# A ranking tower on one core: rounds of eight feature units with one run of sums, in place of two rounds of four

## The chip, the core and the metric

The kernel runs on one core of a Trainium2 chip. The metric is the device time of one execution in microseconds (us). Five engines of the core matter here, each with its own instruction stream: TensorE (PE in the rows, its weight loads PEld), VectorE (DVE), ScalarE (ACT), GpSimd (POOL) and SyncE (SP). They meet through semaphores: an instruction can wait for a count and raise one when it ends.

## The reference, cut to what matters

A batch of 1024 rows; for each row 32 fields are looked up in 32 tables, each entry 64 wide. All 496 pairs of fields are combined through a 64x64 matrix per pair, and a small network follows:

```python
e = jnp.stack([tbl_0[ids[:, 0]], ..., tbl_31[ids[:, 31]]], axis=1)   # 1024 x 32 x 64
p, q = e[:, iu, :], e[:, ju, :]                                       # 496 pairs, iu < ju
z = jnp.einsum('bpe,fpe,bpf->bp', p, kernel, q)                       # 1024 x 496
h = jnp.concatenate([z, dense_ctx], axis=1)                           # 1024 x 512
h = jnp.maximum(h @ W_top1 + b_top1, 0.0)                             # 512 -> 512
h = jnp.maximum(h @ W_top2 + b_top2, 0.0)                             # 512 -> 256
y = h @ W_top3                                                        # 256 -> 1
```

All is 32-bit floating point.

## The kernel before, in words

**Tiles and units.** The batch is cut into 8 tiles of 128 rows. GpSimd gathers the fields (L356), TensorE transposes them into feature layout (a "fill", L611) and ScalarE copies the transposes to `xt` (L394). The pairs of a tile are computed in 32 units of three kinds, all of which take one of three places (`TRING = 3`) in the PSUM ring `t_ps`:

- 16 feature units F (L570): eight matmuls with the pair matrices as weights give the transformed field with features on partitions. VectorE multiplies by the partner field (L476) and writes to a place of `prod`. The sum over the features is still to be made, and lies across partitions: TensorE makes it with matmuls against a matrix of zeros and ones, `sel_sb` (L642, "the sums"), into `z_ps`.
- 8 cross units C (L600) and 8 batch units B (L587), with the batch on partitions. VectorE multiplies them (L498; L517 and L533) into a place of the ring `prod_a`; here the sum lies along a row, and ScalarE makes it (L418), or VectorE (L504), or in the last tile for the C units GpSimd (L374), into `zb`.

The later network is computed for two tiles at a time: `zb` is transposed (L626, "the turn"), then seven "pieces" of matmuls follow (L657, L704, L710), spread between units of later tiles.

**What sets the order.** A table written by the program, `SCHEDULE`, fixes TensorE's instruction order: units, fills, turns, pieces and sums. In tiles 4 to 6 the units run C, F, B, F, eight times over; in tiles 0 to 3 they are sorted by the field that arrives last; in tile 7 they run C, B, F eight times, then the other eight F. ScalarE has its own table made from the same one. VectorE follows the units.

**The sums before the change.** Four F units are a round (`BURST = 4`), so a tile has four rounds and the program 32. The sums of a round are 16 matmuls in a row (L638 to L646), placed five units after the round's last unit (three in the first two tiles), since TensorE first waits for VectorE's products (L632). Those of the last round stand inside the last layers (L670). TensorE's matmul with 32-bit operands shows as two records in the trace, so a run of 16 matmuls is 32 records (x32).

**The places.** `prod` has `FRING = 8` places, two rounds. VectorE, before the first unit of a round, waits for the sums of the round that used these places (L475). `prod_a` has 7 places: a C or B unit waits for the sums of the unit seven before it (L484 to L492). The ring `t_ps` makes TensorE wait, before a unit, for VectorE's product of the unit three before it (L557). `prep_ps` is one buffer for fills, turns and pieces: each waits until ScalarE has copied the one before it (L616, L684).

Of the kernel before, what the change touches and what calls it, by code (L numbers as in the profile page):

```python
# [16 lines left out]
RING = 12  # L17
XRING = 2 * PACKS
TRING = 3
ARING = 7  # L20

# [6 lines left out]
F_UNITS = [x for n, x in enumerate(_UNITS) if n % 3 != 1]  # L30
B_UNITS = [(g, part) for g in range(GROUPS) for part in range(2)]
NF, NC, NBU = len(F_UNITS), len(CROSS_UNITS), len(B_UNITS)
NU = NF + NC + NBU
BURST = 4
FRING = 2 * BURST


def gather_after(t, field):
# [4 lines left out]

ROUNDS = NF // BURST
LAST = TILES * ROUNDS
# [175 lines left out]
TURN_OF = {who: a for a, who in enumerate(TURNS)}  # L221
# [46 lines left out]
def build(nc, ids, tables, kmat, dense, w1, b1, w2, b2, w3, sel, ident, y):  # L268
# [3 lines left out]
    with ctx:  # L272
# [17 lines left out]
        prod = sb("prod", [P, FRING, 2, W])  # L290
        prod_a = sb("prod_a", [P, ARING, 2, W])
        zb = sb("zb", [P, TILES, 2 * P])
# [16 lines left out]
        t_done, prod_done, summed, z_copied = sem("t_done"), sem("prod_done"), sem("summed"), sem("z_copied")  # L309
# [7 lines left out]
        def slot_of(t, k):  # L317

            return (t * PACKS + k) % XRING
# [23 lines left out]
        def _(pool):  # L343
# [17 lines left out]
            for unit in POOL_COUNT:  # L361

                cells, begin = side_cells(unit)
                products = prod_a[:, NTH[unit] % ARING].rearrange("p n (c w) -> p (n c) w", w=EMBED)
                pool.wait_ge(prod_done, COUNT[unit])
# [12 lines left out]
        def _(act):  # L378
# [32 lines left out]
            def sum_bank(*who):  # L411
# [3 lines left out]
                for f in range(cells):  # L415
                    product = prod_a[:, NTH[unit] % ARING, n, f * EMBED:(f + 1) * EMBED]
                    at = begin + n * cells + f
# [49 lines left out]
        @block.vector  # L467
        def _(dve):
            def feature_multiply(t, u):
                r = t * ROUNDS + u // BURST  # L470
                slot, own, here = TURN_OF["F", t, u] % TRING, (t * NF + u) % FRING, slot_of(t, F_UNITS[u][0])
                if r >= 2 and u % BURST == 0:

                    dve.wait_ge(summed, r - 1)
                dve.wait_ge(t_done, COUNT["F", t, u])  # L475
                nc.vector.tensor_tensor(prod[:, own].rearrange("p n (m b) -> p (n m) b", b=P),  # L476
                                        t_ps[:, slot].rearrange("p n (m b) -> p (n m) b", b=P),
                                        xt[:, here:here + 1, :].broadcast_to([P, 2 * GROUP, P]),
                                        ALU.mult).then_inc(prod_done, 1)

            def side_slot(unit):

                n = NTH[unit]
                if n >= ARING:  # L484

# [50 lines left out]
            for unit in UNITS:  # L536
                kind, t, u = unit
# [262 lines left out]
```

## Time and profile before

| | |
|---|---|
| device time, median of 3 runs | 483.64 us (479.96 to 483.74) |
| the profiled execution: its own time | 483.11 us |
| the profiled execution: span of its instructions | 481.3 us |
| granted TensorE clock, mean | 0.957 |
| PE busy | 411.4 us, 85% of the span |
| DVE busy | 342.4 us, 71% |
| ACT busy | 325.4 us, 68% |
| POOL busy | 268.3 us, 56% |

The busy time is a mean over stages: in the first 55 us the tables and matrices arrive and the engines have gaps; from about 57 us to the end TensorE hardly rests. "Idle before" is the time an engine stood still before an instruction and what ended it; "issue" there means that nothing the profile shows was waited for.

### The profile page before, as it was taken

Reading aid. Unit: us, or ns where it says so; the run is one execution under the profiler, and the core shown is the slowest. Engines: PE = TensorE matmul, PEld = TensorE weight load, DVE = VectorE, ACT = ScalarE, POOL = GpSimd, SP = SyncE. Lnnn points to the kernel's source line nnn. Section 1 sums busy time; section 2 is a strip of 40 time slices with the busy share of each in tenths; the row PEclk is TensorE's granted clock in tenths of the full one; section 3 lists DMA queues with packets and bytes.
Section 4 is the critical chain, followed back from the end, with each engine's and each line's share of the span. In section 5 each row is a group of like instructions: output and inputs, shape, how many; then the busy total and the mean of one; then the engine's idle time right before and its main releaser. Section 6 shows DMA issues by size and latency. Waiting matters only on the chain.

```text
span 481.3 us, 12047 instructions
## 1 busy us (share of the span) xinstructions
PE 411.4 (85%) x4144; PEld 280.4 (58%) x4144; DVE 342.4 (71%) x428; ACT 325.4 (68%) x2456; POOL 268.3 (56%) x308
## 2 busy tenths in 40 slices
PE   0554358888898988999999999999999999999997
PEld 0332245655556555767666666666666566666875
DVE  0044158889798878788778887888888788877820
ACT  1244215078967887689857897878786978988512
POOL 5757735566556555555545555556555555577400
PEclk9976568999998999999999999999999999999999
DMA  8751101015111111111111111111111111000000
GB/s 278 268 215 27 26 14 24 18 24 155 21 23 21 20 24 21 21 22 22 23 19 20 23 23 21 20 24 21 20 24 23 22 21 20 16 1 3 1 2 0
DMA packets 12756, 19.17 MB, mean 40 GB/s; under 512 B 6036, under 2 KB 6296, under 8 KB 12568
## 3 DMA queue, kind: packets, MB, share of 16 engines
q0 software_dynamic: 8192, 8.40, 9.4%
q1 hardware_dynamic: 2592, 8.29, 4.8%
q10 hardware_dynamic: 1912, 1.71, 1.2%
q8 instruction: 33, 0.54, 0.5%
q14 instruction: 27, 0.22, 0.1%
HBM read 18.39 MB, written 0.00 MB: 38 GB/s over the span
## 4 chain that ended last, share of the span: by engine, by line
PE 74%; DVE 12%; issue 9%; another core or an unknown queue 2%; DMA 2%; POOL 1%; ACT 1%; DVEq 0%
PE t_ps L570 25%; PE z_ps L642 14%; PE t_ps L600 12%; PE t_ps L587 9%; DVE prod L476 6%; PE prep_ps L657 5%; PE prep_ps L611 3%; DVE prod_a L498 2%; PE prep_ps L704 2%; DVE prod_a L517 2%; PE t_ps L657 2%; DVE zb L504 1%; DMA raw<-tbl,ids_sb 1%; POOL raw L356 1%
## 5 line engine op out<-in xcount | busy, mean ns | idle before, releaser
L356 POOL DMA_INDIRECT raw<-tbl,ids_sb x256 | 242.3, 946 | 172.5 <-issue 48.0
L418 ACT ACTIVATE prod_a<-prod_a 128x64 f32<-128x64 f32 x1184 | 283.9, 243 | 69.0 <-DVE prod_a L533 33.5
L418 ACT ACTIVATION_READ_ACCUMULATOR prod_a<-prod_a 128x1 f32 x1184 | 223.9, 189 | 7.5 <-issue 7.5
L476 DVE TENSOR_TENSOR prod<-t_ps,xt 128x1024 f32<-128x1024 f32 x128 | 155.7, 1220 | 63.6 <-PE t_ps L570 25.5
L570 PEld LDWEIGHTS t_ps<-xt,k_sb 64*128 64x128 f32 x2048 | 136.5, 193 | 55.3 <-issue 31.7
L570 PE MATMUL t_ps<-xt,k_sb 64*128 64x128 f32 x2048 | 151.7, 286 | 19.3 <-issue 10.1
L498 DVE TENSOR_TENSOR prod_a<-t_ps,raw 128x1024 f32<-128x1024 f32 x64 | 78.0, 1219 | 23.6 <-PE t_ps L600 14.7
L600 PE MATMUL t_ps<-k_sb,xt 64*128 64x512 f32 x256 | 74.7, 654 | 19.3 <-issue 14.1
L517 DVE TENSOR_TENSOR prod_a<-t_ps,raw 128x768 f32<-128x768 f32 (+2 forms) x96 | 62.9, 683 | 31.1 <-PE t_ps L587 24.0
L642 PE MATMUL z_ps<-prod,sel_sb 128*32 128x256 f32 x1024 | 71.7, 390 | 4.0 <-issue 3.7
L587 PE MATMUL t_ps<-k_sb,xt 64*128 64x384 f32 (+5 forms) x448 | 66.0, 402 | 3.5 <-issue 1.8
L642 PEld LDWEIGHTS z_ps<-prod,sel_sb 128*32 128x32 f32 x1024 | 33.9, 111 | 39.0 <-issue 22.6
L587 PEld LDWEIGHTS t_ps<-k_sb,xt 64*128 64x128 f32 x448 | 43.0, 191 | 21.9 <-issue 9.6
L394 ACT ACTIVATE xt<-prep_ps 128x512 f32<-128x512 f32 (+2 forms) x47 | 21.0, 446 | 42.6 <-PE prep_ps L611 31.0
L504 DVE TENSOR_REDUCE zb<-prod_a 128x8 f32<-128x512 f32 x76 | 49.7, 676 | 0.0
L611 PE MATMUL prep_ps<-ident_sb,raw 128*128 128x128 f32 x128 | 26.4, 305 | 20.8 <-DMA raw<-tbl,ids_sb 15.1
L600 PEld LDWEIGHTS t_ps<-k_sb,xt 64*128 64x128 f32 x256 | 21.0, 191 | 32.5 <-issue 23.7
L611 PEld LDWEIGHTS prep_ps<-ident_sb,raw 128*128 128x128 f32 x128 | 14.3, 144 | 38.0 <-issue 25.8
L374 POOL TENSOR_TENSOR prod_a<-prod_a 128x512 f32<-128x512 f32 (+4 forms) x40 | 24.3, 607 | 9.7 <-DVE prod_a L498 7.2
L533 DVE TENSOR_TENSOR prod_a<-t_ps,raw 128x128 f32<-128x128 f32 x64 | 18.0, 281 | 0.0
L657 PE MATMUL prep_ps<-zbt,w_sb 128*128 128x256 f32 x48 | 13.6, 405 | 0.0
L657 PE MATMUL prep_ps<-zt,w_sb 128*128 128x256 f32 x48 | 12.3, 379 | 0.0
(30 smaller groups left out, 91.1 us busy)
## 6 DMA issues: line engine op xcount, KB each, us to landing
raw<-tbl,ids_sb POOLq DMA_INDIRECT x256
k_sb<-kmat SPq DMA_DIRECT2D x4, 768.0 KB
k_sb<-kmat SPq DMA_DIRECT2D x4, 512.0 KB
k_sb<-kmat SPq DMA_DIRECT2D x4, 448.0 KB, 4.6
k_sb<-kmat SPq DMA_DIRECT2D x4, 256.0 KB
w_sb<-w ACTq DMA_DIRECT2D x1, 1024.0 KB
w_sb<-w ACTq DMA_DIRECT2D x1, 512.0 KB
ids_sb<-ids SPq DMA_DIRECT2D x1, 128.0 KB, 2.4
```

Source lines behind the costliest of these rows:

```text
L356: nc.gpsimd.indirect_dma_start(raw[:, n % RING, begin:begin + EMBED], None, tables[2 * k + f], bass.IndirectOffsetOnAxis(ap=ids_sb[:, t, 2 ...
L418: last = nc.scalar.activation(product, product, ACT.Copy, accum_out=zb[:, unit[1], at:at + 1])
L476: nc.vector.tensor_tensor(prod[:, own].rearrange("p n (m b) -> p (n m) b", b=P), t_ps[:, slot].rearrange("p n (m b) -> p (n m) b", b=P), x ...
L498: nc.vector.tensor_tensor(out, product, rows.unsqueeze(1).broadcast_to([P, 2, W]), ALU.mult).then_inc(prod_done, 1)
L504: nc.vector.tensor_reduce(zb[:, unit[1], begin + n * cells:begin + (n + 1) * cells], prod_a[:, NTH[unit] % ARING, n, 0:cells * EMBED].rear ...
L517: return nc.vector.tensor_tensor(out[:, :, cols], product[:, :, cols], rows[:, fields * EMBED:(fields + cells) * EMBED].unsqueeze(1).broad ...
L570: last = nc.tensor.matmul(t_ps[:, slot, n, i * P:(i + 1) * P], k_sb[rows, cols], xt[rows, x, :], start=True, stop=True)
L587: last = nc.tensor.matmul(product[:, n, cell * EMBED:(cell + cells) * EMBED], xt[rows, slot_of(t, GROUP * g + field // 2), :], k_sb[rows, ...
L600: last = nc.tensor.matmul(product[:, n, :], xt[rows, slot_of(t, k), :], k_sb[rows, COL["C", k, j]], start=True, stop=True)
L611: last = nc.tensor.transpose(prep_ps[:, n * P:(n + 1) * P], raw[:, group % RING, at * P:(at + 1) * P], ident_sb[:])
L642: last = nc.tensor.matmul(z_ps[32 * group:32 * group + 32, 0:ZBLOCKS * P], sel_sb[:, 30 - 2 * pos:62 - 2 * pos], prod[:, (t * NF + u) % FR ...
L657: return nc.tensor.matmul(out, w1_sb[:, part, m * P:(m + 1) * P], z, start=(part == ZBLOCKS), stop=(part == ZBLOCKS - 1 and half != 0))
```

## The change

A round is now eight F units, so a tile has two rounds and the program 16, each with one run of 32 matmuls. `prod` has 12 places in place of 8, `prod_a` 5 in place of 7 (a place of either is 4 KB per partition). The wait for free places of `prod` is written for a ring that isn't a whole number of rounds: VectorE waits at the 13th F unit and then at every eighth, for the round whose places it is about to reuse.

```diff
@@ constants
-ARING = 7
+ARING = 5
...
-BURST = 4
-FRING = 2 * BURST
+BURST = 8
+FRING = 12
@@ feature_multiply, on VectorE
-                r = t * ROUNDS + u // BURST
-                slot, own, here = TURN_OF["F", t, u] % TRING, (t * NF + u) % FRING, slot_of(t, F_UNITS[u][0])
-                if r >= 2 and u % BURST == 0:
+                n = t * NF + u
+                slot, own, here = TURN_OF["F", t, u] % TRING, n % FRING, slot_of(t, F_UNITS[u][0])
+                if n >= FRING and (n == FRING or n % BURST == FRING % BURST):
 
-                    dve.wait_ge(summed, r - 1)
+                    dve.wait_ge(summed, (n - FRING) // BURST + 1)
```

`ROUNDS`, `LAST` and `ROUND_DONE` follow from `BURST`, and with them `SCHEDULE`. The instructions of VectorE, ScalarE, GpSimd and SyncE stand in the same order; only TensorE's move.

On TensorE in tile 4, before the change, each quarter of a tile has its run of sums (x16) behind a C unit (L600, x2):

```order
L611 MATMUL prep_ps<-ident_sb,raw 128x128 x4
L600 MATMUL t_ps<-k_sb,xt 128x512 x2
L642 MATMUL z_ps<-prod,sel_sb 32x256 x16
L570 MATMUL t_ps<-xt,k_sb 128x128 x8
L587 MATMUL t_ps<-k_sb,xt 128x192
L587 MATMUL t_ps<-k_sb,xt 128x128
L587 MATMUL t_ps<-k_sb,xt 128x256
L587 MATMUL t_ps<-k_sb,xt 128x320
L570 MATMUL t_ps<-xt,k_sb 128x128 x8
```

and now, in the first and then the second quarter of the half tile:

```order
L600 MATMUL t_ps<-k_sb,xt 128x512 x2
L642 MATMUL z_ps<-prod,sel_sb 32x256 x32
L570 MATMUL t_ps<-xt,k_sb 128x128 x8
```

```order
L611 MATMUL prep_ps<-ident_sb,raw 128x128 x4
L600 MATMUL t_ps<-k_sb,xt 128x512 x2
L570 MATMUL t_ps<-xt,k_sb 128x128 x8
L587 MATMUL t_ps<-k_sb,xt 128x192
L587 MATMUL t_ps<-k_sb,xt 128x128
```

Every second run has gone from its place and stands, as 16 more matmuls, in the run that comes two quarters of units later, at the place where the odd rounds had theirs.

At the end of TensorE's stream, before (the turn L626, then the sums of the last round but one, then the last piece of the third pair of tiles L710):

```order
L626 MATMUL prep_ps<-ident_sb,zb 128x128 x4
L642 MATMUL z_ps<-prod,sel_sb 32x256 x16
L710 MATMUL prep_ps<-h,w_sb 1x256 x2
```

```order
L642 MATMUL z_ps<-prod,sel_sb 32x256 x16
L657 MATMUL t_ps<-zt,w_sb 128x128 x8
```

and now:

```order
L626 MATMUL prep_ps<-ident_sb,zb 128x128 x4
L710 MATMUL prep_ps<-h,w_sb 1x256 x2
L657 MATMUL t_ps<-zbt,w_sb 128x256 x2
```

```order
L642 MATMUL z_ps<-prod,sel_sb 32x256 x32
L657 MATMUL t_ps<-zt,w_sb 128x128 x8
```

The run that stood between the turn and L710 is now part of the last one, before the last layers.

## Rows read from the trace of the kernel before

**Rows 1.** The page: busy times, the instruction queue, shares of the chain that ended last.
```profile
PE 411.4 (85%) x4144; PEld 280.4 (58%) x4144; DVE 342.4 (71%) x428; ACT 325.4 (68%) x2456; POOL 268.3 (56%) x308
...
q8 instruction: 33, 0.54, 0.5%
...
PE 74%; DVE 12%; issue 9%; another core or an unknown queue 2%; DMA 2%; POOL 1%; ACT 1%; DVEq 0%
```

**Rows 2.** Busy time in eight quarters (stretch, length, engines' busy us, clock, DMA).
```profile
264.00:277.00 13.00, 12.03 (x132) 7.93 (x134) 11.39 (x15) 10.87 (x84) 7.69 (x9) 1.00 0.11 23
...
sum 105.00, PE 99.61 PEld 69.24 DVE 86.83 ACT 85.55 POOL 60.51; mean PE 12.45 PEld 8.66 DVE 10.85 ACT 10.69 POOL 7.56
```

**Rows 3.** Timeline of PE (start us, length us, line, operation, tiles, records [idle before]).
```profile
258.19 1.13 PE L600 MATMUL t_ps<-k_sb,xt 64*128 64x512 f32 x4
259.16 1.06 PE L570 MATMUL t_ps<-xt,k_sb 64*128 64x128 f32 x16
...
263.16 1.13 PE L600 MATMUL t_ps<-k_sb,xt 64*128 64x512 f32 x4 [0.61 <-DVE prod L476]
264.22 1.93 PE L642 MATMUL z_ps<-prod,sel_sb 128*32 128x256 f32 x32
266.08 0.71 PE L570 MATMUL t_ps<-xt,k_sb 64*128 64x128 f32 x6
267.71 0.81 PE L570 MATMUL t_ps<-xt,k_sb 64*128 64x128 f32 x9 [0.92 <-issue]
```

**Rows 4.** The line of the sums: shortest, median, longest record in ns.
```profile
L642 PE MATMUL z_ps<-prod,sel_sb x1024: 376/379/634, 67.1 to 471.7; 128*32 128x256 f32 x171
```

**Rows 5.** Timeline of PE, at two runs of even rounds.
```profile
329.84 2.73 PE L642 MATMUL z_ps<-prod,sel_sb 128*32 128x256 f32 x32
332.50 1.16 PE L570 MATMUL t_ps<-xt,k_sb 64*128 64x128 f32 x16
...
382.23 3.08 PE L642 MATMUL z_ps<-prod,sel_sb 128*32 128x256 f32 x32
385.25 1.16 PE L570 MATMUL t_ps<-xt,k_sb 64*128 64x128 f32 x16
```

**Rows 6.** Timeline of DVE at a run of sums.
```profile
265.27 1.22 DVE L476 TENSOR_TENSOR prod<-t_ps,xt 128x1024 f32<-128x1024 f32 x1
266.40 1.22 DVE L498 TENSOR_TENSOR prod_a<-t_ps,raw 128x1024 f32<-128x1024 f32 x1
268.67 1.22 DVE L476 TENSOR_TENSOR prod<-t_ps,xt 128x1024 f32<-128x1024 f32 x1 [1.05 <-PE t_ps L570]
```

**Rows 7.** Timeline of PE in tile 0, at the first two runs of sums.
```profile
67.11 2.41 PE L642 MATMUL z_ps<-prod,sel_sb 128*32 128x256 f32 x32
...
76.96 1.13 PE L600 MATMUL t_ps<-k_sb,xt 64*128 64x512 f32 x4 [2.25 <-issue]
...
81.75 1.93 PE L642 MATMUL z_ps<-prod,sel_sb 128*32 128x256 f32 x32
```

**Rows 8.** Timeline of PE at the end.
```profile
454.13 1.93 PE L642 MATMUL z_ps<-prod,sel_sb 128*32 128x256 f32 x32
...
461.44 0.66 PE L626 MATMUL prep_ps<-ident_sb,zb 128*128 128x128 f32 x4 [0.57 <-ACT h L436]
462.02 1.93 PE L642 MATMUL z_ps<-prod,sel_sb 128*32 128x256 f32 x32
463.77 1.03 PE L710 MATMUL prep_ps<-h,w_sb 128*1 128x256 f32 x4
```

**Rows 9.** ScalarE's copy of the turned sums, by tile (shortest, median, longest ns).
```profile
L401 ACT ACTIVATE zbt<-prep_ps x4: 571/587/597, 177.9 to 462.1; 128x512 f32<-128x512 f32 x4
```

**Rows 10.** Timeline of DVE, the last F units.
```profile
456.14 4.62 DVE L476 TENSOR_TENSOR prod<-t_ps,xt 128x1024 f32<-128x1024 f32 x4 [0.89 <-PE z_ps L642]
```

**Rows 11.** ScalarE's last sum of a B unit; DVE's product five C and B units later.
```profile
111.72 0.18 ACT L418 ACTIVATION_READ_ACCUMULATOR prod_a<-prod_a 128x1 f32 x1
...
114.69 1.22 DVE L498 TENSOR_TENSOR prod_a<-t_ps,raw 128x1024 f32<-128x1024 f32 x1
```

## The prediction, made before the changed kernel ran

> **What bounds the kernel now.** I read the page first: TensorE is busy for 411 of 481 us and holds 74% of the chain that ended last, VectorE 12% [rows 1]. The shares are means over stages, so the next view is the busy time by stretch. Between 264 and 369 us lie eight quarters of a tile, 13.1 us each (105 / 8). In one, TensorE is busy 12.45 us, VectorE 10.85, ScalarE 10.69 [rows 2]. TensorE is the bound, but VectorE is only 2.3 us behind it, and this gap is about as long as the part of a quarter in which TensorE does sums and therefore makes nothing for VectorE. That is what the reader should keep in mind: the two engines share a ring of three places, and the sums are the breathing space of one and a pause of the other.
>
> The timeline of TensorE shows a run of sums in detail [rows 3]. It starts 1.06 us after the start of the C unit ahead of it; an F unit behind a C unit starts after 0.97 us (258.19 to 259.16). The first record of the run and the last are 1.93 - 0.38 = 1.55 us apart [rows 3, 4], so 0.050 us from one to the next, and the next F unit starts 1.86 us after the run's start. 32 records at 0.050 are 1.60 us; 0.26 us more pass before the F unit starts. So a run costs 1.60 us of work, 0.26 us to get out and 0.09 us to get in.
>
> There is a third thing, which the profile does not explain. Close behind the start of a run TensorE stands still for most of a microsecond, with nothing waited for ("issue"): here 0.92 us after the first six records of the F unit [rows 3], in other runs in the middle of the sums, which then take 2.66 us (329.84 to 332.50) or 3.02 us (382.23 to 385.25) in place of 1.86 [rows 5], so 0.80 and 1.16 us too long. I call it the hiccup. Of the runs between 264 and 411 us each has one; the runs of tiles 2 and 3 that stand behind a B unit have little of it, and the runs from 421 us on none, as 454.13 and 462.02 show [rows 8].
>
> **The change part by part.** Sixteen runs of 32 matmuls replace 32 of 16. The matmuls, their weight loads and all other instructions stay.
>
> *Getting in and out.* Each merged pair saves 0.26 + 0.09 = 0.35 us. Fourteen pairs lie between tile 0 and the tail, where TensorE sets the pace: 14 x 0.35 = 4.9 us. For this the trace agrees with a rule of the Trainium skill (TensorEngine Tiling (Array Packing), Tiling Modes) that changing the tiling mode drains TensorE; the sums are 128 rows by 32 columns and the units 64 by 128. The page gives no figure for that. TensorE: Matmul & The Clock Gate (Single matmul latency, the Trainium skill) has about 0.175 us for an unhidden drain; by that figure alone the estimate of this term would be 14 x 0.175 = 2.5 us, and by the rows it is 4.9.
>
> *The hiccups.* The runs that go are those of even rounds. Eight of them carry a hiccup, of 0.98 us in the mean of the two shown [rows 5]. If it belongs to the run, eight go: 7.8 us. If it belongs to a number of instructions, none goes. A doubled run could also have two. The ends are thus 7.8 us and nothing. I take 7.8, because in tile 4 to 6 each hiccup stands within 40 records of a run's start, and where no run is near there is none of that length.
>
> *What VectorE gives back.* Without its run and its hiccup a quarter costs TensorE 13.1 - 1.86 - 0.98 = 10.3 us. VectorE needs 10.85 [rows 2]. TensorE can be no more than three units ahead, and is already at that limit when the next sums come: the C unit ahead of them waited 0.61 us for VectorE's product [rows 3]. So the quarter without sums goes at VectorE's pace, 10.85 - 10.27 = 0.58 us longer. In the eight half tiles where a hiccup goes, that is 4.6 us back. In the others the quarter keeps more than 10.85 us of TensorE's work, and nothing is given back. The ends: nothing, if VectorE's slack evens out, and what the last rival below says.
>
> *The first pair.* The first run, at 67.11, costs nothing now: at 76.96 TensorE waits 2.25 us for something that arrives, and would wait longer without the run. Its 32 records move to 81.75 and stand on the path there [rows 7]: +1.6 us.
>
> *The tail.* The run between the turn (L626) and L710 goes. L710 writes the buffer that ScalarE copies after the turn, and the copy takes 0.59 us [rows 9]. Now the run hides it: from the turn's start to L710 are 2.33 us (461.44 to 463.77) [rows 8]. After the change they are the turn's 0.66, the copy's 0.59 and two hand-overs, which I take as 0.05 each: 1.35 us, 0.98 less. The 32 records stand in the last run instead, +1.6 us. Together +0.6 us. The run at 454.13 doubles too, and VectorE's last four products wait for its end, as now with 0.89 us [rows 10]; they are needed only by the very last run, over 9 us later (456.14 + 4.62 = 460.8 against 470), so that costs nothing while this cover of 9 us holds.
>
> *The places.* VectorE's wait for `prod` never holds it longer than TensorE does, since the sums stand at least two units ahead of the unit that waits for them, and VectorE needs those two units anyway; the exception is the one at the end, above. Queued behind that waiting product are VectorE's last three alone. With 5 places in place of 7 a product needs ScalarE's sums of the unit five before it. The narrowest place is in tile 1: the sum ends at 111.90 and the product starts at 114.69, 2.8 us later [rows 11]; in tiles 4 to 6 there are some 10 us. The cost is nothing; if the cover went, ScalarE's 10.69 us a quarter would come in as a third bound, still under VectorE's.
>
> *The sum.* -4.9 - 7.8 + 4.6 + 1.6 + 0.6 = -5.9 us, on the profiled execution's own 483.1: 477.2. The median of the three runs is 0.5 us above that execution, so I forecast 477.7 us.
>
> **The rivals.** About 1% (4.8 us) is what a measurement can tell from no change: under 478.8 is faster, over 488.5 slower.
>
> 1. *The hiccup comes once in so many instructions.* Their number does not change, so none goes, and the quarters without sums keep 11.2 us of TensorE's work, over VectorE's 10.85: nothing is given back either. -4.9 + 2.2 = -2.7: 480.9 us. For it: 33 packets of instructions of 16 KB were loaded [rows 1], about one for each of the 32 runs. Against: all runs from 421 us on have none. The Trainium skill (Runtime: NRT & Kernel Launch, Instruction fetch mechanics) says that code comes in such blocks of 256 instructions and that the cost of crossing into one is mostly hidden; the trace agrees on the blocks and can't say whether they are the hiccups. Chance 0.24.
>
> 2. *VectorE gives nothing back.* Its 2.3 us of idle time a quarter could let it work off what TensorE piles up, since TensorE's halt during the doubled run comes later but is longer. -4.9 - 7.8 + 2.2 = -10.5: 473.1 us. For it: over the eight quarters TensorE waits for VectorE but a few tenths each. Against: that wait stands just where the next sums stood. Chance 0.15.
>
> 3. *VectorE starves in the long run* (the one on the other side). At a run's start three units lie ready for it; from 264.22 to 267.62 (266.40 + 1.22) it has work, 3.4 us [rows 3, 6]. Now sums of 1.86 and the next unit's 1.1 are 2.96 us: covered, and the idle 1.05 at 268.67 [rows 6] is the hiccup's. After the change, 1.86 + 1.60 + 1.1 = 4.56 us: 1.16 us are uncovered. This decides if VectorE, and not TensorE, sets the time between the runs all along, that is, if the pause in TensorE's output is longer than 3.4 us and the ring is full before each. Then thirteen half tiles lose 1.16 us each, 15.1, and 7.8 of hiccups and the getting in and out are all that speaks against it: 15.1 - 7.8 + 2.2 = +9.5: 493.1 us. Against: VectorE's 10.85 leave 2.3 us of each quarter. Chance 0.14.
>
> 4. *Five places are too few*, so that VectorE waits for ScalarE: by rows 11 it would take a ScalarE 2.8 us later than now. Chance 0.03, some 486 us. That the change does not do what it says is excluded by TensorE's order, which has the 16 runs.
>
> **How the numbers follow.** My forecast has 0.38, and 0.06 is for what I don't see. The range of the forecast alone is 474 to 481 (half of the hiccups, or half of what is given back). To hold eight in ten it must take in rivals 1 and 2 and leave out most of 3: 471 to 487. Faster by over 1%: rival 2 and some two thirds of the forecast, 0.42. Within 1%: rival 1 and the rest of the forecast, 0.42. Slower: rival 3 and a little of the unseen, 0.16.
>
> **What would show it.** In the changed profile: a run of 64 records whose first and last start about 3.15 us apart, one per half tile; a hiccup at each of them and none in the quarters between (right for the second term), or one there too (rival 1); in the quarters without sums TensorE's idle time ahead of C units "until DVE prod" grown to over half a microsecond (the give-back); VectorE idle once per half tile for some 2 us, waiting for TensorE. ScalarE's sums must not show up as what VectorE waits for. At the end L710 should start 1.35 us after the turn. I am wrong if hiccups are longer in long runs, or if VectorE's idle time as a whole grows.

## The result, and the profile after

The changed kernel takes 497.0 us (median of 4 runs, 496.26 to 497.60), the kernel before in the same session 483.25 us (4 runs, 479.96 to 483.74). The ratio is 1.032, with a 95% interval of 1.029 to 1.035: 3.2% slower. I had forecast 477.7 us and a range up to 487.

The page of the changed kernel, in lines that answer to [rows 1]:

```profile
span 495.8 us, 12034 instructions
PE 414.8 (84%) x4144; PEld 282.8 (57%) x4144; DVE 340.6 (69%) x428; ACT 325.8 (66%) x2456; POOL 267.6 (54%) x308
PE 68%; DVE 15%; issue 10%; POOL 4%; DMA 2%; ACT 0%; DVEq 0%; another core or an unknown queue 0%
```

Of its groups the one of VectorE's feature products, before and then now (line, engine, operation, count | busy us, mean ns | idle us before it and what ended most of that):

```profile
L476 DVE TENSOR_TENSOR prod<-t_ps,xt 128x1024 f32<-128x1024 f32 x128 | 155.7, 1220 | 63.6 <-PE t_ps L570 25.5
L476 DVE TENSOR_TENSOR prod<-t_ps,xt 128x1024 f32<-128x1024 f32 x128 | 155.5, 1219 | 76.1 <-PE t_ps L570 40.1
```

The work is the same, and no engine's busy time grew by more than 1%. What grew is idle time: on TensorE from 69.9 to 81.0 us (the span less its busy time), on VectorE from 138.9 to 155.2. Of VectorE's, this group had 63.6 us before the change, 25.5 of them until an F unit, and has 76.1 and 40.1 now. In the same stretch as [rows 2], 264 to 369 us, less work gets done by both engines, 82.43 us of VectorE's against 86.83:

```profile
sum 105.00, PE 97.92 PEld 67.10 DVE 82.43 ACT 83.54 POOL 57.66; mean PE 48.96 PEld 33.55 DVE 41.21 ACT 41.77 POOL 28.83
```

The timeline of TensorE over one half tile, which answers to [rows 3]:

```profile
271.81 5.40 PE L642 MATMUL z_ps<-prod,sel_sb 128*32 128x256 f32 x64
277.14 1.16 PE L570 MATMUL t_ps<-xt,k_sb 64*128 64x128 f32 x16
...
288.82 1.03 PE L587 MATMUL t_ps<-k_sb,xt 64*128 64x192 f32 x8 [0.66 <-DVE prod L476]
...
293.44 1.16 PE L570 MATMUL t_ps<-xt,k_sb 64*128 64x128 f32 x16 [0.68 <-DVE prod_a L533]
...
296.53 1.16 PE L570 MATMUL t_ps<-xt,k_sb 64*128 64x128 f32 x16 [0.88 <-issue]
...
299.27 4.68 PE L642 MATMUL z_ps<-prod,sel_sb 128*32 128x256 f32 x64
```

One run of 64 records per half tile is there, but it takes 5.33 us to the next unit (271.81 to 277.14) and then 4.61, where 3.6 would do (the same run takes 3.59 us in after_again, below): the hiccups did not go, they stand inside the doubled runs. Between the runs TensorE waits for VectorE at 288.82 and 293.44. The gap at 296.53 is called "issue", but it ends 0.06 us after VectorE's product of the C unit three units before (from 295.25 to 296.47), and that product had itself waited 0.73 us for ScalarE's sums of `prod_a`. The timeline of VectorE in the same half tile, answering to [rows 6]:

```profile
274.19 1.22 DVE L498 TENSOR_TENSOR prod_a<-t_ps,raw 128x1024 f32<-128x1024 f32 x1
278.35 1.22 DVE L476 TENSOR_TENSOR prod<-t_ps,xt 128x1024 f32<-128x1024 f32 x1 [2.94 <-PE t_ps L570]
```

VectorE stands still for 2.94 us at this run and for 2.95 at the next (305.09): once per half tile, until the F unit behind the sums.

### The profile page after: what moved, and what is told of

Its sections match the earlier page's. It is cut to its first block, busy times and chain, and to the rows that moved or that the text cites. A ratio compares the mean times of both kernels' runs of the same rounds, so it can differ in the third digit from the quotient of the medians.

```text
span 495.8 us, 12034 instructions
## 1 busy us (share of the span) xinstructions
PE 414.8 (84%) x4144; PEld 282.8 (57%) x4144; DVE 340.6 (69%) x428; ACT 325.8 (66%) x2456; POOL 267.6 (54%) x308
## 4 chain that ended last, share of the span: by engine, by line
PE 68%; DVE 15%; issue 10%; POOL 4%; DMA 2%; ACT 0%; DVEq 0%; another core or an unknown queue 0%
PE t_ps L570 22%; PE z_ps L642 14%; PE t_ps L600 13%; PE t_ps L587 7%; DVE prod L476 7%; PE prep_ps L657 4%; DVE prod_a L498 4%; PE prep_ps L611 3%; POOL raw L356 3%; DVE zb L504 2%; PE prep_ps L704 2%; DVE prod_a L517 2%; POOL prod_a L374 2%; PE t_ps L657 2%; DMA raw<-tbl,ids_sb 1%
## 5 line engine op out<-in xcount | busy, mean ns | idle before, releaser
L418 ACT ACTIVATE prod_a<-prod_a 128x64 f32<-128x64 f32 x1184 | 283.8, 243 | 71.7 <-DVE prod_a L533 32.3
L418 ACT ACTIVATION_READ_ACCUMULATOR prod_a<-prod_a 128x1 f32 x1184 | 223.9, 189 | 8.8 <-issue 8.8
L476 DVE TENSOR_TENSOR prod<-t_ps,xt 128x1024 f32<-128x1024 f32 x128 | 155.5, 1219 | 76.1 <-PE t_ps L570 40.1
L570 PEld LDWEIGHTS t_ps<-xt,k_sb 64*128 64x128 f32 x2048 | 133.0, 195 | 61.1 <-issue 29.2
L570 PE MATMUL t_ps<-xt,k_sb 64*128 64x128 f32 x2048 | 149.5, 288 | 19.3 <-issue 6.7
L600 PE MATMUL t_ps<-k_sb,xt 64*128 64x512 f32 x256 | 75.0, 664 | 25.3 <-issue 19.1
L587 PE MATMUL t_ps<-k_sb,xt 64*128 64x384 f32 (+4 forms) x448 | 65.7, 408 | 9.1 <-DVE prod L476 7.7
L642 PE MATMUL z_ps<-prod,sel_sb 128*32 128x256 f32 x1024 | 68.7, 382 | 5.0 <-issue 3.9
L587 PEld LDWEIGHTS t_ps<-k_sb,xt 64*128 64x128 f32 x448 | 42.8, 192 | 27.5 <-DVE prod L476 11.0
L642 PEld LDWEIGHTS z_ps<-prod,sel_sb 128*32 128x32 f32 x1024 | 37.9, 109 | 34.0 <-issue 20.2
L504 DVE TENSOR_REDUCE zb<-prod_a 128x8 f32<-128x512 f32 x76 | 49.7, 676 | 0.0
L394 ACT ACTIVATE xt<-prep_ps 128x512 f32<-128x512 f32 (+2 forms) x47 | 20.9, 445 | 40.6 <-PE prep_ps L611 19.5
L600 PEld LDWEIGHTS t_ps<-k_sb,xt 64*128 64x128 f32 x256 | 20.0, 191 | 40.1 <-issue 30.0
L409 ACT ACTIVATE zt<-z_ps 128x256 f32<-128x256 f32 x8 | 3.1, 384 | 17.6 <-PE z_ps L642 17.5
```

The lines of the kernel that those rows point to most:

```text
L418: last = nc.scalar.activation(product, product, ACT.Copy, accum_out=zb[:, unit[1], at:at + 1])
L504: nc.vector.tensor_reduce(zb[:, unit[1], begin + n * cells:begin + (n + 1) * cells], prod_a[:, NTH[unit] % ARING, n, 0:cells * EMBED].rear ...
L570: last = nc.tensor.matmul(t_ps[:, slot, n, i * P:(i + 1) * P], k_sb[rows, cols], xt[rows, x, :], start=True, stop=True)
L587: last = nc.tensor.matmul(product[:, n, cell * EMBED:(cell + cells) * EMBED], xt[rows, slot_of(t, GROUP * g + field // 2), :], k_sb[rows, ...
L600: last = nc.tensor.matmul(product[:, n, :], xt[rows, slot_of(t, k), :], k_sb[rows, COL["C", k, j]], start=True, stop=True)
L642: last = nc.tensor.matmul(z_ps[32 * group:32 * group + 32, 0:ZBLOCKS * P], sel_sb[:, 30 - 2 * pos:62 - 2 * pos], prod[:, (t * NF + u) % FR ...
```

## The experiments

They ran later, in groups on four chips, and this matters for two things. On each of the four the kernel before takes 420.5 to 421.5 us, not 483; I call the chip of the first profiles, which has no number on record, the first chip, and these the later chips. And their profiles have next to no hiccups: of the runs of sums between 100 and 400 us only one is too long, by 0.78 us (in before_light_both, at 177.90). So the readings of the hiccups (H1 to H4 where an expectation names them) could not be told apart. The loss could be studied: its ratio is about the same, 1.032 on the first chip and 1.028 later, with intervals that overlap. All ratios are to the kernel before on the same chip, with 95% intervals; times of different groups differ by up to 1 us for the same kernel, so between groups I compare ratios. The ideas to be told apart are that the long pause in TensorE's output starves VectorE (my rival 3; A in the expectations), that a ring is too short or that the hiccups grew (both called B there), that the long run costs TensorE something by itself (C, and later E), and that ScalarE's copy of the finished sums holds the other engines up (D).

**The changed kernel again** (after_again), with no edit.

> The changed kernel again, beside the others. Theory A (VectorE stands still in the doubled run; TensorE's unexplained halts have little part in the loss): 1.027 to 1.032 of the kernel before, also where the profile shows no halts. Theory B (the halts grew in the doubled runs and make the loss): with no halts in the profile the ratio falls under 1.02.

432.58 us, ratio 1.028 [1.025, 1.031]. Its timelines of TensorE, then of VectorE:

```profile
296.69 3.66 PE L642 MATMUL z_ps<-prod,sel_sb 128*32 128x256 f32 x64
300.28 1.16 PE L570 MATMUL t_ps<-xt,k_sb 64*128 64x128 f32 x16
...
320.89 3.66 PE L642 MATMUL z_ps<-prod,sel_sb 128*32 128x256 f32 x64
```

```profile
298.24 1.22 DVE L498 TENSOR_TENSOR prod_a<-t_ps,raw 128x1024 f32<-128x1024 f32 x1
301.49 1.22 DVE L476 TENSOR_TENSOR prod<-t_ps,xt 128x1024 f32<-128x1024 f32 x1 [2.04 <-PE t_ps L570]
...
306.20 1.22 DVE L498 TENSOR_TENSOR prod_a<-t_ps,raw 128x1024 f32<-128x1024 f32 x1 [0.63 <-PE t_ps L600]
...
316.79 1.22 DVE L498 TENSOR_TENSOR prod_a<-t_ps,raw 128x1024 f32<-128x1024 f32 x1 [0.33 <-PE t_ps L600]
```

The runs are clean (3.66 us), and the kernel is slower by about the same share as on the first chip, as A expected. The hiccups are not needed for the loss. VectorE waits 2.04 us at the run; then, from 306.20 to 316.45, it has no gap at all: the quarter without sums goes at VectorE's pace. It shows on TensorE and VectorE side by side:

```profile
311.40 1.03 PE L587 MATMUL t_ps<-k_sb,xt 64*128 64x192 f32 x8
312.53 1.16 PE L570 MATMUL t_ps<-xt,k_sb 64*128 64x128 f32 x16
```

```profile
310.13 1.21 DVE L476 TENSOR_TENSOR prod<-t_ps,xt 128x1024 f32<-128x1024 f32 x1
311.26 1.21 DVE L498 TENSOR_TENSOR prod_a<-t_ps,raw 128x1024 f32<-128x1024 f32 x1
```

Each of the two units starts 0.06 us after VectorE's product of the unit three before it (which ends at 311.34 and 312.47), since only then is its place in `t_ps` free. The half tile takes 24.20 us (296.69 to 320.89).

**The places.** Two kernels: rounds of four with the new rings and the new wait (b4_f12_a5), and the changed kernel with the old 7 places of `prod_a`, paid for with the ring of gathered fields (b8_a7_raw8).

```diff
@@ against the kernel before; the wait at L475 is the changed kernel's, too
-ARING = 7
+ARING = 5
...
-FRING = 2 * BURST
+FRING = 12
```

> The changed kernel with rounds of four again, so 32 runs of 16 matmuls, but its rings kept: 12 places for prod, 5 for prod_a. Theory A (the doubled run is the loss: VectorE uses up its three waiting units and then stands still): the time of the kernel before, 483.3 us, within 1.5. Theory B (five places are too few, VectorE waits for ScalarE): most of the loss stays, 490 to 497 us.

421.19 us, 0.999 [0.998, 1.000], as A expected. The rings and the wait alone cost nothing.

```diff
@@ against the changed kernel
-RING = 12
+RING = 8
...
-ARING = 5
+ARING = 7
```

> The changed kernel with 7 places for prod_a again; room for them comes from the ring of gathered rows, 8 groups in place of 12. Theory A: 494 to 497 us, since the 3.5 us in which VectorE waits for ScalarE in the changed kernel's profile are mostly given back by TensorE's halt. Theory B: about 485 us. If it is slower than 497, the smaller ring of gathered rows costs something itself.

432.64 us, 1.028 [1.025, 1.030], the same as the changed kernel. So the places of `prod_a` are not the cause. Whether 12 places of `prod` are too few for rounds of eight no run tests, but the trace answers it: in after_again VectorE waits for TensorE's sums (L642) not once between 40 and 400 us, and in the changed kernel on the first chip once, for 2.6 us. What is left is the length of the rounds. b4_f12_a5 also shows what a half tile is with rounds of four, on TensorE:

```profile
255.10 1.93 PE L642 MATMUL z_ps<-prod,sel_sb 128*32 128x256 f32 x32
...
266.99 1.93 PE L642 MATMUL z_ps<-prod,sel_sb 128*32 128x256 f32 x32
...
278.88 1.94 PE L642 MATMUL z_ps<-prod,sel_sb 128*32 128x256 f32 x32
```

23.78 us (255.10 to 278.88), 0.42 less than with the doubled run, although TensorE has one run more to get in and out of.

That is not yet the whole loss, which is 10.4 us between these two profiles. Where it arises is seen from the start of the F unit behind the same run of sums in both, counted in doubled runs. after_again is 0.3 us behind at the first (in tile 0), 4.0 at the fourth (in tile 2), 5.6 at the eighth (in tile 4), 9.8 at the 14th (in tile 7) and 10.4 at the end. In the six half tiles from the eighth run to the 14th it loses 0.42 or 0.43 us in four, and 1.25 in each of the two that have the turn (L626).

**Two pauses close together, no longer run** (b4_lag7). The kernel before, with its sums seven units behind the round in place of five.

```diff
-SUMS_LAG = 5
+SUMS_LAG = 7
```

> The kernel before with its sums two units later (SUMS_LAG 7 in place of 5), so in tiles 4 to 6 each run stands behind a B unit and not behind a C unit. Theory H3 (a halt appears where the instructions ahead of the run are few and fast, since the runs of tiles 2 and 3 behind a B unit had little of it): the halts shrink in tiles 4 to 6, 472 to 478 us. Theory H4 (the halt belongs to the run or to time, wherever it stands): 482 to 485 us.

433.41 us, 1.028 [1.026, 1.031]. It was made to sort out the hiccups, and neither H3 nor H4 foresaw a loss; the reading that follows came after the result. TensorE, then VectorE:

```profile
274.91 1.93 PE L642 MATMUL z_ps<-prod,sel_sb 128*32 128x256 f32 x32
276.78 1.16 PE L570 MATMUL t_ps<-xt,k_sb 64*128 64x128 f32 x16
277.87 1.13 PE L657 MATMUL prep_ps<-zbt,w_sb 128*128 128x256 f32 x4
278.83 1.03 PE L657 MATMUL prep_ps<-zt,w_sb 128*128 128x256 f32 x4
279.79 1.13 PE L600 MATMUL t_ps<-k_sb,xt 64*128 64x512 f32 x4
```

```profile
277.99 1.23 DVE L476 TENSOR_TENSOR prod<-t_ps,xt 128x1024 f32<-128x1024 f32 x1
281.04 1.23 DVE L498 TENSOR_TENSOR prod_a<-t_ps,raw 128x1024 f32<-128x1024 f32 x1 [1.83 <-PE t_ps L600]
```

The sums (1.87 us) and the piece (1.92 us) now have a single F unit between them, and VectorE waits 1.83 us behind them. Runs, their number and all rings are as before, and the loss is as large as that of the change. That the two are equal is chance: here the first two tiles lose nothing, since their sums did not move, and in tile 5 two quarters take 25.16 us (274.91 to the run at 300.07) against 23.78. What costs is a stretch in which TensorE makes little for VectorE, whatever fills it.

**Gathers left out in tiles 4 to 7** (before_nogather4), aimed at the hiccups.

```diff
+GATHERED = 4
...
+                if t >= GATHERED:
+                    continue
```

TensorE's wait for these gathers goes with them.

> The kernel before without the gathers of tiles 4 to 7 (it leaves them out and computes those tiles from rows that older tiles left); TensorE's instructions are the same but for the waits for them. Theory H1 (TensorE's halts without a releaser, 0.8 to 1.2 us behind each run of sums from 264 to 411 us, come from something the gathers do, since the runs after the gathers' end have none): those halts are gone in tiles 4 to 6, some 11 us less, about 472 us. Theory H2 (they belong to TensorE's own stream of instructions, its code blocks or its queue): they stay, 481 to 484 us.

421.08 us, 0.999 [0.997, 1.001]. There were no hiccups on its chip to take away, so it decides nothing on them. It shows that in tiles 4 to 7 the gathers do not bound.

**VectorE made lighter** (before_light_dve and after_light_dve). The same edit in both: VectorE's 76 row sums (L504, 49.7 us in all) become additions of one element per cell.

```diff
-                nc.vector.tensor_reduce(zb[...], prod_a[...], mybir.AxisListType.X, ALU.add)
+                first = prod_a[...][:, :, 0:1]
+                nc.vector.tensor_tensor(zb[...].unsqueeze(2), first, first, ALU.add)
```

> The kernel before with VectorE's 76 row sums (L504, 0.65 us each) replaced by a sum over one element of each cell, which takes them out of the result. Theory A: TensorE sets the pace before the change, so the 45 us less of VectorE's work shorten the program by little: 0.97 to 1.0 of the kernel before.

> The same in the changed kernel. Theory A (the loss is VectorE's: its work between the doubled runs and its pause in them): with VectorE 1.3 us lighter per quarter TensorE alone sets the pace, the doubled runs save 0.35 us each, and this kernel is no slower than before_light_dve, from 6 us faster to 1 us slower. Theory C (the loss is TensorE's own, in the long run itself): it stays about 12 us slower than before_light_dve.

413.88 us, 0.982 [0.978, 0.986], and 418.91 us, 0.995 [0.991, 0.998]. With a lighter VectorE the doubled rounds lose 5.0 us in place of 12.0 (432.58 less the 420.53 of the kernel before in this group): about 7 are VectorE's. Neither reading came true: A expected at most 1 us of loss, C 12. The kernel before gains 7 too, so VectorE bounded it in part already.

The other 5 us can be read in the same profile. TensorE's waits between 40 and 400 us that ScalarE ended, and one of them in tile 4, at the fill behind a turn:

```profile
PE prep_ps L610 <- ACT zbt L401: 2.7, 3, 1.4
PE prep_ps L610 <- ACT xt L394: 2.7, 3, 1.9
```

```profile
236.29 0.66 PE L610 MATMUL prep_ps<-ident_sb,raw 128*128 128x128 f32 x4 [1.38 <-ACT zbt L401]
```

With the smaller ones these waits are 7.6 us, against 2.3 in before_light_dve. `prep_ps` is one buffer, and each fill waits until ScalarE has copied what was in it; ScalarE's copies (L394, L401) stand in its queue between its row sums, and come late. In tiles 4 to 6 after_light_dve wins 0.08 or 0.09 us in each of the four half tiles without a turn and loses 1.72 and 1.44 in the two with one.

**ScalarE lighter as well** (before_light_both and after_light_both): ScalarE's row sums (L418) also become one copy of one element per cell.

```diff
-                for f in range(cells):
-                    last = nc.scalar.activation(product, product, ACT.Copy, accum_out=zb[...])
+                nc.scalar.activation(zb[...].unsqueeze(2), first, ACT.Copy)
```

> The kernel before with the row sums of VectorE and of ScalarE both replaced (VectorE: a sum over one element of each cell; ScalarE: one copy of one element of each cell), which leaves these sums out of the result. TensorE is then the only busy engine: a few us under before_light_dve, 405 to 413.

> The same in the changed kernel. Theory A+ (TensorE's saving of 0.35 us per merged pair is real, and what turned it into a loss are VectorE and ScalarE, both too busy to make up a long pause): 1 to 5 us faster than before_light_both (sum of TensorE's terms: -4.9 + 2.2 = -2.7). Theory E (the price per run is not real, or the doubled run costs TensorE something by itself): 0 to 4 us slower.

411.65 us, 0.979 [0.976, 0.981], and 412.02 us, 0.980 [0.978, 0.982]. The two are equal: with light partners the loss is gone. But the gain that I had priced does not come either: A expected 1 to 5 us, and 0.4 us slower lies in E's range. In part this is the early tiles, where with light partners TensorE waits for gathered fields (2.2 us at 174.89 in before_light_both alone): from the seventh run to the 15th the changed kernel is 0.9 to 1.2 us ahead. Half tiles of TensorE, first of before_light_both, then of after_light_both (the lines of the kernel are three lower here):

```profile
234.11 1.93 PE L639 MATMUL z_ps<-prod,sel_sb 128*32 128x256 f32 x32
...
257.88 1.50 PE L639 MATMUL z_ps<-prod,sel_sb 128*32 128x256 f32 x23
```

```profile
255.15 3.66 PE L639 MATMUL z_ps<-prod,sel_sb 128*32 128x256 f32 x64
258.74 1.16 PE L567 MATMUL t_ps<-xt,k_sb 64*128 64x128 f32 x16
259.74 0.93 PE L584 MATMUL t_ps<-k_sb,xt 64*128 64x192 f32 x8
260.49 1.06 PE L567 MATMUL t_ps<-xt,k_sb 64*128 64x128 f32 x16
...
268.67 1.06 PE L567 MATMUL t_ps<-xt,k_sb 64*128 64x128 f32 x16
269.56 0.93 PE L584 MATMUL t_ps<-k_sb,xt 64*128 64x192 f32 x8
270.47 1.16 PE L567 MATMUL t_ps<-xt,k_sb 64*128 64x128 f32 x16
...
278.84 1.50 PE L639 MATMUL z_ps<-prod,sel_sb 128*32 128x256 f32 x24
```

23.77 us against 23.69: 0.08 saved per half tile, not 0.35. The merged run takes 3.59 us (255.15 to 258.74), 0.13 less than two of 1.86; a C unit without a run behind it takes 0.09 less, and an F unit without a run ahead of it takes 0.89 (268.67 to 269.56) in place of 1.00 (258.74 to 259.74). That is 0.33 in all. But 0.25 of it is lost again in the quarter without sums, which takes 10.17 us (268.67 to 278.84) where 11.89 - 1.86 - 0.11 = 9.92 would be due. It can be seen: the B unit of 269.56 takes 0.91 us to the F unit behind it, the same kind at 259.74 only 0.75, and that F unit 1.09 to the piece at 271.56, in place of 1.00 (260.49 to 261.49). The F unit at 270.47 starts 0.05 us after VectorE's product of the C unit three before it ends (at 270.42), so TensorE is still held by VectorE here. VectorE's timeline at the run:

```profile
255.68 1.22 DVE L496 TENSOR_TENSOR prod_a<-t_ps,raw 128x1024 f32<-128x1024 f32 x1
259.95 1.22 DVE L474 TENSOR_TENSOR prod<-t_ps,xt 128x1024 f32<-128x1024 f32 x1 [3.06 <-PE t_ps L567]
```

However fast it is, it cannot work ahead of TensorE; it stands still for 3.06 us and must make the products of two quarters in what is left.

**ScalarE's copy of the finished sums** (D). ScalarE copies them (L409) at one place of its own order, and waits there for TensorE's run. In three kernels that place is three entries later; the third of them is b4_lag4, which follows below, with the same move.

```diff
+Z_LATER = 3
+for _n in reversed([n for n, x in enumerate(SCALAR_SCHEDULE) if x[0] == "sums" and x[1] % ROUNDS == ROUNDS - 1]):
+    _x = SCALAR_SCHEDULE.pop(_n)
+    SCALAR_SCHEDULE.insert(_n + Z_LATER, _x)
```

> The changed kernel with ScalarE's copy of z_ps (L409, which waits for the end of a tile's last run of sums) three places later in ScalarE's order. Theory D (part of the loss: the doubled run holds ScalarE's queue at this copy, and fills and sums behind it come late to TensorE): 2 to 4 us faster than the changed kernel, about 1.020 of the kernel before. If ScalarE's hold costs nothing: 1.027 as before.

> after_light_dve (changed kernel, VectorE's row sums replaced by a sum over one element of each cell) with the same move of ScalarE's copy. Theory D with theory A: both holds are gone and only TensorE's own account is left, 14 changes of tiling mode less at 0.35 us against 2.2 us at the program's two ends: 410 to 414 us where before_light_dve takes 413.9. If it stays at 419, something else holds TensorE.

> The faster version so far (the kernel before with SUMS_LAG 4, 0.994 of the kernel before) with the same move of ScalarE's copy. A run of 16 matmuls holds ScalarE half as long, and there are four runs a tile: theory D says 0 to 1.5 us faster than with SUMS_LAG 4 alone, 0.990 to 0.995 of the kernel before.

In the changed kernel 433.12 us, 1.029 [1.027, 1.031]: no gain where 1.020 was expected, so the idea falls. With light VectorE 417.19, 0.992 [0.989, 0.994], against 0.995 [0.991, 0.998] without the move: the intervals overlap, and the 410 to 414 us expected are missed. Its waits for ScalarE's copy of the turn are as long as before (2.7 us). In b4_lag4 418.15, 0.993 [0.991, 0.996], against 0.994: nothing.

**Sums where they help** (b4_lag4): the kernel before with its sums four units behind the round. They then stand in front of the fill and the C unit, not between C and F.

```diff
-SUMS_LAG = 5
+SUMS_LAG = 4
```

> The kernel before with its sums one unit earlier (SUMS_LAG 4), so that in tiles 4 to 6 they stand directly beside a fill and ahead of the C unit, where they stood behind it. If the place among the other work without products (fills, pieces) decides, as the run with SUMS_LAG 7 says (12 us slower, with the sums one unit ahead of a piece): the pauses lie three units from the next piece, one change of tiling mode less per run, 2 to 5 us faster. If a longer pause (sums 1.9 and fill 0.6 us) already starves VectorE: 2 to 6 us slower.

418.26 us, 0.994 [0.993, 0.996]: faster than both kernels, by the 2 to 5 us that the first reading expected and not the loss of 2 to 6 that the second allowed. TensorE:

```profile
262.47 1.93 PE L642 MATMUL z_ps<-prod,sel_sb 128*32 128x256 f32 x32
264.33 0.66 PE L611 MATMUL prep_ps<-ident_sb,raw 128*128 128x128 f32 x4
264.92 1.13 PE L600 MATMUL t_ps<-k_sb,xt 64*128 64x512 f32 x4
265.88 1.06 PE L570 MATMUL t_ps<-xt,k_sb 64*128 64x128 f32 x16
...
274.17 1.93 PE L642 MATMUL z_ps<-prod,sel_sb 128*32 128x256 f32 x32
```

11.70 us a quarter (262.47 to 274.17) against 11.89 (266.99 to 278.88 in b4_f12_a5). The fill already breaks the row of units, and a run beside it needs one break less: C to F takes 0.96 us (264.92 to 265.88), and no run stands between them.

**The same in the changed kernel** (b8_lag4, the same edit).

> The changed kernel with SUMS_LAG 4, so that the doubled run stands beside the fill, ahead of the C unit. If the gain of that place is a change of tiling mode less (0.35 us or so per run, as many as runs), half as many runs give half of it: 1 to 1.5 us faster than the changed kernel. If the place helps VectorE, more: 1.02 of the kernel before or less. Theory A says the pause now has the fill's 0.6 us on top of 3.5, so it could as well be 2 to 5 us slower than the changed kernel.

429.78 us, 1.020 [1.017, 1.023], where the changed kernel has 1.028. The place is worth some 3 us here too, more than the 1 to 1.5 expected with half as many runs. A half tile takes 24.02 us (from the run at 268.79 to the one at 292.81), 0.18 less than in after_again, which is the gain of the place once; the two half tiles with a turn gain 0.6 and 0.4. Most of the loss stays.

**Shorter rounds** (b2): rounds of two units, 64 runs of 8 matmuls, 8 and 7 places.

```diff
@@ against the kernel before; the wait at L475 is the changed kernel's
-BURST = 4
-FRING = 2 * BURST
+BURST = 2
+FRING = 8
```

> Rounds of two feature units (64 runs of 8 matmuls; prod 8 places, prod_a 7). The price per run alone: 32 more runs at 0.35 us, 11 us slower than the kernel before, 1.027. If a shorter pause helps VectorE and ScalarE beyond what the kernel before has, less: 1.01 to 1.02. If the price per run is not real: 1.0 or faster.

419.56 us, 0.998 [0.997, 1.000]. In tile 5, on TensorE:

```profile
264.32 1.07 PE L642 MATMUL z_ps<-prod,sel_sb 128*32 128x256 f32 x16
...
271.05 1.07 PE L642 MATMUL z_ps<-prod,sel_sb 128*32 128x256 f32 x16
...
276.54 1.07 PE L642 MATMUL z_ps<-prod,sel_sb 128*32 128x256 f32 x16
```

A quarter takes 12.22 us (264.32 to 276.54) with two runs of 8, 11.89 with one of 16. One run more costs 0.33 us, with the number of matmuls unchanged: this is the price per run that I had read as 0.35. By that price alone the kernel would be at 1.027; it is level with b4_f12_a5 (0.998 and 0.999). In the profiles the last product of tile 3 ends 4.3 us earlier (211.64 against 215.92), 2.8 of them in tile 0, where kernels with the same order of work already differ by up to 1.6. So shorter pauses in tiles 0 to 3 may be what pays for the runs; how much they are worth, no run parts.

**Both kinds of place** (b2_lag4: b2 with its sums four units behind; b2_then_4: rounds of two, but from tile 4 the runs of two rounds stand together, four units behind).

```diff
@@ against b2; b2_lag4 has the first pair of lines only
-SUMS_LAG = 5
+SUMS_LAG = 4
+PAIRED_FROM = 4
...
+        paired = r // ROUNDS >= PAIRED_FROM and r % 2 == 0 and r + 1 < LAST - 1
+        done = ROUND_DONE[r + 1 if paired else r]
```

> Rounds of two in all tiles, with SUMS_LAG 4. Against b2_then_4 it has 16 more runs: at 0.35 us each some 5 us slower in tiles 4 to 7, unless half of its runs, which stand ahead of a C unit and behind no fill, cost less.

> Rounds of two in tiles 0 to 3; from tile 4 on the sums of two rounds stand together (16 matmuls), beside the fill (SUMS_LAG 4); the last run is of 8 matmuls. If a short pause is worth 4 us in the early tiles, the place beside the fill some 2 us, and a short last run 0.8 us: 413 to 416 us, 0.982 to 0.989 of the kernel before, faster than SUMS_LAG 4 alone (0.994). If the gains are the same gain twice: 0.990 to 0.995.

418.75 us, 0.995 [0.993, 0.997], and 417.29 us, 0.992 [0.990, 0.994]. The second is the fastest kernel of this study that leaves nothing out, 0.8% under the kernel before; against b4_lag4 (0.994 [0.993, 0.996]) the intervals overlap. It lies in the range of "the same gain twice", not in that of the full sum of the gains, and b2_lag4 is 1.5 us slower, not 5.

## Why the prediction was wrong, step by step

The sum was -5.9 us, and the time moved by +13.8. Two of its terms failed. The hiccups were to go and stayed, which took away what made the sum a gain; and what VectorE gives back, put at 4.6 us, is several times as much, which made it a loss.

**Getting in and out, -4.9.** The price was right: 0.35 us per run as I worked it out, 0.33 in b2 (0.13 of it in the run, 0.09 ahead of it, 0.11 in the F unit behind it, as the rows of after_light_both part it). It was not collected. It is TensorE's time, and in the changed kernel the half tile is not TensorE's alone: 24.20 us, where 23.78 - 0.35 = 23.43 were expected; even with both partners light only 0.08 is left of it. The Trainium skill (TensorEngine Tiling (Array Packing), Tiling Modes) says only that a change of mode drains TensorE, and gives no price. The traces agree that going from the units to the sums and back costs time beyond the matmuls, 0.33 to 0.35 us for both ways together.

**The hiccups, -7.8.** This step failed. They do not belong to a run so that one goes with each run removed: in the changed kernel's profile the 12 doubled runs from 104 to 408 us hold some 15 us of them, where the 20 or so runs of the kernel before had some 18. So some 3 us went, not 7.8. Rival 1, with none gone, was nearer. The error of this term is about 5 us; that the ratio is about the same on chips without hiccups says that the loss does not need them.

**What VectorE gives back, +4.6.** This is the step that decided, and it was mis-sized because it was written for half of the cycle. On the later chips, where no hiccups blur the sum, the loss of 12.0 us is -4.9 for getting in and out, +0.9 for the two ends (0.3 and 0.6, below) and so some 16 us for what the partners give back (an estimate, from these three numbers); the light kernels put about 5 of them on ScalarE, for which the prediction had nothing. I priced the quarter without sums (VectorE's 10.85 over TensorE's 10.27) and took the other quarter as TensorE's, with a pause that VectorE absorbs. Rival 3 has the other half: in the long run VectorE has 3.4 us of work, the pause is 3.6 and the F unit's 1.1, and 1.16 us lie open in each half tile. I gave it 0.14 and 493.1 us. In the profile the open piece is 2.04 us without hiccups and 2.94 with them, more than 1.16: the ring holds only 2.77 us of VectorE's work when the run begins (296.69 to 299.46 in after_again), not 3.4. Waits of 0.6 to 0.7 us of TensorE for VectorE stand in the quarter without sums, as forecast, though at B and F units and not at the C units that I had named.

Rival 3 has the right place, but its price was near by luck. It charges the open piece in full. Over a half tile VectorE has 21.2 us of work in after_again, and with 2.04 + 0.96 us of standing still that is the 24.20 measured; in b4_f12_a5 it has 21.3 us of work and already stands still for 2.5, 1.2 of them behind the two runs. So the long run adds 0.8 us of standing still behind the sums, 0.3 is regained elsewhere, and the half tile is 0.42 us longer. This also answers what I had written against the rival, that VectorE's 10.85 leave 2.3 us of each quarter: about half of such idle time stands behind the sums, where VectorE can't use it to work ahead.

after_again shows the loss without hiccups, b4_f12_a5 and b8_a7_raw8 free the rings, the light kernels take the loss away in two steps (7 of 12 us with VectorE, the rest with ScalarE as well), and b4_lag7 makes a loss of that size with the runs as they were. ScalarE comes in because it is as loaded as VectorE (21.11 us of work in the half tile of after_again, VectorE 21.19) and its copies out of `prep_ps` come late to TensorE, as the waits of after_light_dve show; moving its other copy, of the finished sums, did not help, and two places more in `prod_a` neither.

**The first pair and the tail.** In the tail of the first chip's changed kernel, on TensorE, which answers to [rows 8]:

```profile
475.23 0.66 PE L626 MATMUL prep_ps<-ident_sb,zb 128*128 128x128 f32 x4 [0.56 <-ACT h L436]
476.57 1.02 PE L710 MATMUL prep_ps<-h,w_sb 128*1 128x256 f32 x4 [0.69 <-ACT zbt L401]
```

L710 starts 1.34 us after the turn; 1.35 was forecast. From the F unit behind the 14th doubled run to the end after_again takes 0.6 us longer than b4_f12_a5, and the tail was put at +0.6. The first pair was put at +1.6: the F unit behind the run there (at 81.10 now, 81.75 before) comes 1.07 us later on the first chip (84.69 against 83.62), and 0.3 on the later ones. **The places** cost nothing on the later chips (b4_f12_a5, b8_a7_raw8). On the first chip VectorE came to wait for ScalarE's sums five times, 3.5 us in all, which the prediction had ruled out, and at 296.53 one of these waits reached TensorE; what they cost there no run shows.

**The gain of a deeper ring** wasn't tried. A unit fills 128x1024 f32, 4 KB per partition, so three of them are 12 KB; the Trainium skill (PSUM — Partial Sum Buffer, Specifications (TRN2)) gives 16 KB per partition in 8 banks of 2 KB. The other two, `prep_ps` and `z_ps`, have to fit in what is left. No run here tests that limit.

## What to carry to other kernels

Before you make one engine's side work rarer and longer, compare the longest stretch in which it makes nothing for its partner with the work that the ring between them holds, and ask whether the partner has time to spare in the rest of the cycle: a mean share of 83% of a quarter looked like slack, but much of the idle time stood at the pauses themselves. Here the stretch was longer than the ring, and merging cost more than the changes of mode it saved; halving the rounds left the time where it was, and putting the pauses where the engine changes mode anyway gained 0.6%. Two short pauses one unit apart counted as one long one. And look at every partner: a third engine with nearly as much work held TensorE through a single buffer.

## What the runs showed of the hardware

- The same kernel took 483 us on the first chip and 420.5 to 421.5 on four later ones, at granted clocks of 0.957 (the profiled execution) and 0.984 to 1.000. Against b4_f12_a5, which is as fast as the kernel before, the last product of tile 0 ends 26 us later on the first chip (103.14 and 77.29), the hiccups are some 18 us, and the rest was not traced.
- TensorE's halts of about a microsecond, with nothing waited for, stood in the profiles of the first chip near most runs of sums; between 100 and 400 us the profiles of the later chips have one run that is too long. They are thus no property of the code alone, nor of a number of instructions alone. What they are stays open.
- A run of sums less or more changes a quarter by 0.33 us with the matmuls unchanged; a run beside a transposition, which already breaks the row of units, costs 0.19 us less than one between two units (11.70 us a quarter in b4_lag4, 11.89 in b4_f12_a5).
